# A graph-aggregation MLP layer on one core: float32 rows of h behind the gather, split on chip in batches of three chunks, the edge search and the first dense tile moved ahead of the branch

## What is computed

```
# x (3125,256) float32; 50,000 edges src -> dst, sorted by dst
h   = relu(layernorm(x))
agg = segment_sum(h[src], dst, 3125) + h
h1  = agg @ W1 + b1                       # (3125, 1024)
h1  = relu(batchnorm over the 3125 rows(h1) * gamma + beta)
out = x + relu(h1 @ W2 + b2)              # (3125, 256)
```

## Time and profile before

| | before |
|---|---|
| median of 3 runs | 427.06 us (425.68 to 458.85) |
| the profiled execution | 428.42 us, its span 426.5 us |
| mean granted TensorE clock | 0.98 |
| busy: PE, DVE, ACT, POOL | 85%, 48%, 45%, 49% of the span |
| DMA moved | 71.26 MB |

### The profile page before, as it was taken

One profiled execution on the slowest core, in us unless ns is written; L12 is line 12 of the kernel. 1 busy time (PEld: TensorE's weight loads), 2 busy tenths in 40 slices (PEclk: granted clock), 3 DMA queues, 4 the chain that ended last, 5 costly groups with the idle time before them and its releaser, 6 DMA issues.

```text
span 426.5 us, 5346 instructions
## 1 busy us (share of the span) xinstructions
PE 362.8 (85%) x1797; PEld 305.3 (72%) x1797; DVE 203.6 (48%) x513; ACT 190.1 (45%) x398; POOL 208.9 (49%) x226
## 2 busy tenths in 40 slices
PE   0103599999999999999999999945689899999995
PEld 0102488888888788888888888823468788888884
DVE  5895856546655555466555554310235521212122
ACT  1891344444444444445444443300235799991000
POOL 6580177667776767776776777774700000000000
PEclk9999999999999999999999999975999999999999
DMA  7669877767776777776676777787820003222211
GB/s 178 160 187 289 278 226 219 200 172 203 225 201 190 207 201 204 204 219 196 178 190 184 203 219 211 207 269 227 244 73 2 0 17 98 84 70 80 78 37 51
DMA packets 27054, 71.26 MB, mean 167 GB/s; under 512 B 4540, under 2 KB 11985, under 8 KB 26397
## 3 DMA queue, kind: packets, MB, share of 16 engines
q0 software_dynamic: 15504, 49.80, 40.9%
q1 hardware_dynamic: 11518, 21.06, 17.1%
HBM read 61.24 MB, written 9.60 MB: 166 GB/s over the span
## 4 chain that ended last, share of the span: by engine, by line
PE 75%; DMA 11%; POOL 5%; DVE 4%; issue 2%; ACT 2%; SPq 0%; DVEq 0%; ACTq 0%; POOLq 0%
PE ps L541 20%; PE ps L521 18%; PE ps L616 17%; PE ps L628 9%; PE ps L577 8%; DMA g_ring<-h_rows,gsrc 8%; POOL scratch L448 3%; DMA scratch<-in_src,scratch 3%; POOL g_ring L491 2%; DMA scratch<-in_x 1%; PE ps L530 1%; DVE oh L902 1%; PE ps L604 1%; ACT scratch L705 1%; DVE picks L994 0%
## 5 line engine op out<-in xcount | busy, mean ns | idle before, releaser
L491 POOL DMA_INDIRECT g_ring<-h_rows,gsrc x187 | 186.4, 997 | 90.2 <-issue 40.8
L616 PE MATMUL ps<-hp,counts 125*125 125x512 f32 x350 | 110.1, 432 | 0.0
L521 PE MATMUL ps<-hT,w 128*128 128x250 f32 (+1 forms) x416 | 98.5, 370 | 0.2
L902 DVE TENSOR_TENSOR oh<-iota,tab 128x500 bf16<-128x500 bf16 x196 | 73.4, 417 | 31.0 <-PE ps L577 30.1
L541 PE MATMUL ps<-w,h 128*125 128x256 f32 x400 | 86.7, 379 | 1.0 <-ACT h L743 1.0
L521 PEld LDWEIGHTS ps<-hT,w 128*128 128x128 f32 x416 | 76.4, 192 | 12.0 <-ACT h L678 1.1
L678 ACT ACTIVATE h<-ps,vec 128x250 f32<-128x250 f32 (+1 forms) x104 | 48.1, 463 | 81.6 <-PE ps L521 81.2
L724 ACT ACTIVATE counts<-ps 125x500 fp32r<-125x500 f32 (+1 forms) x98 | 54.7, 560 | 66.8 <-PE ps L577 65.1
L628 PE MATMUL ps<-g_ring,picks 128*125 128x512 f32 x187 | 70.2, 447 | 16.6 <-DMA g_ring<-h_rows,gsrc 14.8
L541 PEld LDWEIGHTS ps<-w,h 128*125 128x125 f32 x400 | 74.8, 188 | 12.7 <-issue 1.2
L949 DVE BATCH_NORM_STATS2 bst<-h 128x6 f32<-128x250 f32 (+1 forms) x104 | 42.5, 410 | 76.4 <-ACT h L678 75.7
(11 more groups left out here) (97 smaller groups left out, 125.3 us busy)
## 6 DMA issues: line engine op xcount, KB each, us to landing
h_rows<-hp SPq DMA_DIRECT2D x5, 1120.0 KB
x<-in_x SPq DMA_DIRECT2D x12, 250.0 KB
out<-o SPq DMA_DIRECT2D x12, 250.0 KB
g_ring<-h_rows,gsrc POOLq DMA_INDIRECT x187, 3.8
scratch<-in_x SPq DMA_DIRECT2D x5, 560.0 KB
hd<-h_rows SPq DMA_DIRECT2D x11, 224.0 KB
w<-in_L_gnn_W SPq DMA_DIRECT2D x2, 1024.0 KB, 9.0
h_rows<-hp SPq DMA_DIRECT2D x5, 130.0 KB
```

The costliest lines, as they stand in the source:

```text
L491: pool.indirect_dma_start(g_ring[:, c % GQ, :].bitcast(F32), None, h_words, bass.IndirectOffsetOnAxis(ap=gsrc[:, c:c + 1], axis=0)).then_i ...
L521: last = pe.matmul(p_hid[w % 2][:, 0:n], w1[:, f, k * P:(k + 1) * P], hT[:, buffer, f, 0:n], start=(f == 0), stop=(f == KD - 1))
L616: last = pe.matmul(p_sum[d], counts[:, d % 2, t, :], hp[:, t, :, :].rearrange("p s d -> p (s d)"), start=(t == 0), stop=(t == NT - 1))
L902: last = dve.tensor_tensor(oh[:, b % OB, v, :].rearrange("p (k g) -> p k g", g=CG), iota4[:, :, :], keys, ALU.is_equal)
```

## The change

1. `h_rows` holds one float32 row per node (1 KB instead of 2 KB). SP stores `h32`, no longer waiting for the halves. `hd`, the own rows, is float32 too and has one buffer; own rows are added by a float32 matmul after the first chunk.
2. The gather ring has 3 slots of 3 chunks (YQ, YN). A tile's 17 chunks make batches of 3, 3, 3, 3, 3, 2. ACT copies a landed batch to its rounded half (`split_hi`), DVE subtracts for the rest (`split_lo`) into `halves` (two buffers), and PE sums from there. POOL may gather batch y when batch y-3 has been split. `picks` are made per batch.
3. The search for the first edges has no gathers: all dst are loaded (125 rows of 400, and the next 100), DVE compares every 100th with the starts, PE finds the chunk and sums, DVE compares in it. The two last x loads wait no longer for it. Keys are ordered differently, so `group_keys` has four DVE operations in place of eight.
4. The order of DVE's head changes: one-hots 0 to 6 come before `gather_tables`, and the counts and dense work of slots 7 to 13 (tile 0) are run before the flag is read. POOL gathers the first 9 chunks before the flag.
5. `plan()` places splits as well as chunks. Evaluated, the new plan has 142 of 187 chunks, the same 72 units and the splits of batches 0 to 50 (of 66) in slots 0 to 104; the last chunk is in slot 124, and 90 units are placed by then. Of those 51 batches, 27 have their first chunk in the slot right after their split.

```diff
-YB = (5, 4, 4, 4)
+YB = (3, 3, 3, 3, 3, 2)
+YQ = 3
-T_ROWS, T_GATHER, T_LAND = 3500, 1250, 3700
+T_ROWS, T_GATHER, T_LAND, T_SPLIT = -6000, 1300, 3700, 2500
+EARLY = 2 * CB
...
+        while z >= EARLY and y < NG * len(YB) and len(s.splits) < 2 and (y < 2 or used.get(y - 2, z) < z):
+            free = usable[y - YQ] if y >= YQ else T_ROWS
+            landed = max(issued, free) + T_GATHER * len(chunks_of_batch(y)) + T_LAND
+            if landed > now and not idle:
                 break
...
+            usable[y] = now + T_SPLIT
...
+            if v not in usable or v in s.splits or usable[v] > now and not idle:
...
-    h_rows = nc.dram_tensor("h_rows", [N, 2 * D], F32R).ap()
+    h_rows = nc.dram_tensor("h_rows", [N, D], F32).ap()
...
+            sp.dma_start(dst_e[0:NP - 1, :], bass.AP(tensor=dst.tensor, offset=0, ap=[[EP, NP - 1], [1, EP + CE]])
+                         ).then_inc(s_dst, 16)
...
-                sp.wait_ge(s_hi, g + 1)
-                sp.wait_ge(s_lo, g + 1)
+                sp.wait_ge(s_h32, g + 1)
...
+            def gather(c):
+                y, i = batch_of_chunk(c)
+                if i == 0 and y >= YQ:
+                    pool.wait_ge(s_split, y - YQ + 1)
+                pool.indirect_dma_start(g_ring[:, y % YQ, i, :], None, h_rows, ...
...
+            for s in SLOTS[CB:EARLY]:
+                count(s.count)
+                dense(*s.dense)
...
+            def split_hi(y):
+                n = len(chunks_of_batch(y))
+                act.wait_ge(s_gath[y % YQ], landed_by(y))
+                if y >= 2:
+                    act.wait_ge(s_chunk, chunks_of_batch(y - 2)[-1] + 1)
+                act.activation(halves[:, y % 2, 0:n, 0, :], g_ring[:, y % YQ, 0:n, :], ACT.Copy).then_inc(s_ghi, 1)
...
+                    for y in s.splits:
+                        split_hi(y)
...
+            def chunks_above():
+                dve.wait_ge(s_dst, 32)
+                chain(dve.tensor_copy(nexts[:, :], ...))
+                for j in range(SB):
+                    last = dve.tensor_scalar(above[:, j, :], vrow[0:NP, :], nexts[:, j:j + 1], None, ALU.is_le)
+                dve.tensor_tensor(steps[:, :, :]..., dst_e[:, 0:EP], dst_e[:, CE:EP + CE], ALU.subtract)
+            def smaller():
+                dve.scalar_tensor_tensor(less[:, :], p_rows, PAD_DST, vrow[0:CE, :], ALU.add, ALU.is_lt)
...
+                def split_lo(y):
+                    dve.wait_ge(s_ghi, y + 1)
+                    dve.tensor_tensor(halves[:, y % 2, 0:n, 1, :], g_ring[:, y % YQ, 0:n, :],
+                                      halves[:, y % 2, 0:n, 0, :].bitcast(F32), ALU.subtract).then_inc(s_split, 1)
```

More of the change, by code:

```diff
@@ L94, in chunks_of_batch, with landed_by @@
     return range(a, a + YB[v])
+def landed_by(y):
+    return 16 * sum(len(chunks_of_batch(v)) for v in range(y % YQ, y + 1, YQ))
 def plan():
@@ L112, in plan @@
     tiles, blocks, ready, todo, placed = [], [], {}, [], 0
-    used = []
-    z, now, c, gate, landed = CB, 0, 0, 0, T_ROWS + T_LAND
+    z, now, c, gate = CB, 0, 0, EARLY
+    y, issued, used, usable = 0, T_ROWS, {}, {}
     while placed < UNITS:
@@ L117, in plan @@
         finished = []
-        while c < NC and z >= gate and len(s.chunks) < 4:
-            if z < end and landed > now:
+        idle = z >= end and not todo
+        while z >= EARLY and y < NG * len(YB) and len(s.splits) < 2 and (y < 2 or used.get(y - 2, z) < z):
+            free = usable[y - YQ] if y >= YQ else T_ROWS
+            landed = max(issued, free) + T_GATHER * len(chunks_of_batch(y)) + T_LAND
+            if landed > now and not idle:
                 break
             now = max(now, landed)
+            issued = landed - T_LAND
+            s.splits.append(y)
+            usable[y] = now + T_SPLIT
+            y += 1
+        while c < NC and z >= gate and len(s.chunks) < 4:
+            v = batch_of_chunk(c)[0]
+            if v not in usable or v in s.splits or usable[v] > now and not idle:
+                break
+            now = max(now, usable[v]) + T_CHUNK
             s.chunks.append(c)
-            used.append(now)
+            used[v] = z
             c += 1
@@ L157, in plan @@
         z += 1
+        if z == EARLY:
+            now = 0
     assert blocks[-3:] == list(range(NBLK - 3, NBLK)), blocks
-    for y in range(NG * len(YB)):
-        z = CB if y < 2 else next(i for i, s in enumerate(slots) if chunks_of_batch(y - 1)[0] in s.chunks)
-        at(z).picks.append(y)
+    for v in range(NG * len(YB)):
+        z = EARLY if v < 2 else next(i for i, s in enumerate(slots) if chunks_of_batch(v - 1)[0] in s.chunks)
+        at(z).picks.append(v)
     return slots, tiles, blocks
+FIRST_C = chunks_of_batch(YQ)[0]
 SLOTS, TILES, BLOCKS = plan()
@@ L235, in build @@
         vrow = cut(LANES)
[L236 to L247, removed]
+        vrow_r = cut(GROUPS)
+        dst_e = cut(EP + CE, NP).bitcast(I32)
+        nexts = cut(SB, NP)
         win_i = cut(WB).bitcast(I32)
@@ L666, in _ @@
                     for s in range(n):
[L667 removed]
+                        last = pe.matmul(ps[0:NP, s, 0:D], zeros, g_any[:, 4 + s, :], start=False, stop=True)
                     last.then_inc(s_gclose, 1)
@@ L781, in _ @@
                     for s in range(n):
-                        copy_low(act, tiles + s, ps[0:NP, s, :])
+                        act.activation(low[:, :], ps[0:NP, s, 0:D], ACT.Copy).then_inc(s_low, 1)
                         if m:
@@ L1006, in _ @@
                         onehots(s.count + OB)
+                    for y in s.splits:
+                        split_lo(y)
                     for y in s.picks:
```

350 lines of the change are left out of this document (174 added, 176 removed).

## The result

The changed kernel takes **441.92 us** (median of 4, 440.42 to 443.99) against 427.0 of the kernel before on the same chip: ratio **1.0376** [1.0343, 1.0409], slower. Ratios here compare fast executions alone (of the four of before, the one of 458.85 us was in the chip's slower state), so they aren't exactly the quotient of the medians. The profiled execution took 440.42 us with a span of 438.6, 12.1 more than before. The forecast of 433 had the sign and missed 9 us of the size: 441.92 lies inside the stated 422 to 446, but above the 427 to 439 of the forecast itself.

A forecast was written before the change was run, and what follows sets the result against it. PE was taken as the bound from 50.04 to 279.6 us, then gathers. Dense end 279.6 - 6.6 + 1.5 - 5.0 + 4 = 273.5, plus 55.5 and 13.0 to 342.0, plus 90.9: span 432.9, time 433 us, range 422 to 446.

The forecast's parts named there:

- the forecast itself: The case in which the forecast's own steps hold: 427 to 439 us, chance 0.48.
- The head: Before dense work: without search gathers and with half the store, dense work starts at 43.4 us, 6.6 earlier.
- The bubble: Slots 7 to 13 and slot 14: cover sum, the flag's matmul and the branch add 1.5 us (0 to 3).
- The middle: Slots 0 to 104: 20 fewer chunks give -5.0 us, waits for the new splits +4 (0 to 13).
- one own-rows matmul fewer, 0.4: Slots 0 to 104: a saving of 0.4 us on PE, counted within the -5.0 for fewer chunks.
- DVE and ACT become the clock of the middle: Rival, chance 0.17: split chain too long in 27 tight batches; PE waits 13 to 20 us, not 4: 443 to 449.
- Behind slot 104: After the last dense matmul: 36 gathers at POOL's 1.25 us each make the stretch 55.5 us (50 to 62).
- The end: Last gather to last chunk summed: landing 2.6, hi and lo of two chunks 1.5, two matmuls 0.5 us.
- the change delivers its gain: Rival, chance 0.17: head 10 earlier, no bubble or split waits, 50 us behind slot 104: 418.5; half of each, 423.
- The port rule "in full": Rival, chance 0.10: behind slot 104 splits and picks hold gathers throughout, 18 us instead of 4: 447; with half, 440.
- The early search: Rival, chance 0.08: the early search doesn't move the dense start, which comes only 2 us earlier: 437.5.
- a smaller row buys "nothing": Gathers behind slot 104: POOL's pace stays 0.95 + 0.30 us each, so halving the row gains nothing.

The follow-up runs named there:

- r5: The kernel before with only the new edge search, head order and tile 0 before the flag; old 2 KB rows and ring, no splits: 424.91 us, ratio 0.9974.
- r1: The kernel before with one planner constant changed (T_GATHER 1250 to 1500), so 135 chunks instead of 162 in slots 0 to 104: 445.85 us, ratio 1.0439.
- r9: The changed kernel with T_LAND 2700 and T_SPLIT 3500: still 142 early chunks, but 5 tight batches instead of 27: 436.02 us, ratio 1.0244.
- r4: The changed kernel without DVE's subtraction for the low half (left zero); POOL and PE wait for ACT's copy instead: 430.4 us, ratio 1.0099.
- r8: r3 with picks made by one DVE operation with one SBUF tensor input per chunk, instead of one two-input operation per batch: 428.7 us, ratio 1.0067.
- r7: The kernel before, each gather fetching only the rounded halves (1 KB a row), low halves zero; order, ring, store and head unchanged: 423.61 us, ratio 0.9932.
- r3: The changed kernel with T_ROWS -11000, T_LAND 2200, T_SPLIT 3500: 151 early chunks instead of 142, 2 tight batches instead of 27: 428.54 us, ratio 1.0055.

## Why the prediction missed its size

**The head held.** Dense work starts at 43.13 for a forecast of 43.4. Two terms erred against each other: the load of all dst landed at 7.54, not 5.0, and DVE's chain with its waits took 35.6 us instead of 37.8 plus the count. The bubble of +1.5 put into slots 7 to 13 and the branch didn't come (9.91 us, before 9.83). r5 shows what the head is worth alone: 4.8 us of start, 3.5 of span, and by the median 1.6 us, which its interval doesn't tell from none.

**The middle is the step that failed**: "New are per batch ... I take 0.15 each: +4 (0 to 13)", against -5.0 for the 20 chunks. The single operations were priced within 0.05 us, and DVE is at 72% (159.77 of 223.26) for a forecast of 77. What was wrong is the sum. The chunks were worth more than taken, 0.33 each by r1, so -6.6; from slot 14 on the stretch grew by 3.4 instead of shrinking, so what the change adds there is 10.0 us, not 4. Only 5.0 of them are waits that the view shows (6.8 less 1.8). The other five lie inside what the rows count as busy, where ends are modelled: PE's busy time is 216.44 for 20 chunks fewer, 217.66 before. Some 1.1 of them are a term that the forecast had with the wrong sign, "one own-rows matmul fewer, 0.4": in float32 the own rows of nine tiles are 18 matmuls and 5.4 us busy (L607), where those of ten were 10 matmuls and 4.7 us (L604).

r9 and r4 say where more of the ten comes from: room between split and chunk takes 4.3 us off, leaving out `split_lo` takes 4.2 off, and both end at 219.0. By r1's price 142 chunks without splits would be at 213.3; 5.7 are left in each. PE's waits there are 4.6 us in r9 (3.9 for picks) and 4.5 in r4 (3.5 for picks), 2.8 and 2.7 more than before; the own rows are 1.1; the last 1.8 or so have no experiment of their own, and stay open.

The rival "DVE and ACT become the clock of the middle" described this mechanism, in tight batches. It set 13 to 20 us for it and came too high, as the forecast came too low; the time stands between them. The sign that the forecast named for it, PE waiting over 8 us for splits, didn't show: by the view it waits 6.8, and the rest of the cost isn't seen as waits.

**Behind slot 104** the decisive step held: 57.6 us for 55.5, gathers at POOL's pace. Of its terms: 37 gathers started there, not 36; their stretch over 0.947 us is 2.8 us, not 4; to the end of the last gather it is 50.5 us, where 36 at 1.25 with the stretch, the start and the stretched landing made 51.0. The 6.69 us landing came as expected and cost POOL 1.3 beyond its 0.30. The end was too short: "landing 2.6, hi and lo 1.5, two matmuls 0.5", 4.6 us, against 7.07, since the last splits stood behind units, in part at half clock. After the last chunk 13.7 us for 13.0, the rest 91.0 for 90.9.

**The sum.** Against 433.4: head -0.3, slots 7 to 13 -1.5, middle +4.6, tail +2.1, units +0.7, rest and outside the span about 0; that is, to 0.1, the 440.4 of the profiled execution less 434.8. That the profiled execution stands only 5.6 us off is in part luck: head and bubble erred by 1.8 the other way. The last 2.9 us are the step from it to the median: this profiled execution was the fastest of the four (440.42, median 441.92), where the forecast carried over the ratio of before and took 1.4 off.

**The other rivals.** That the change delivers its gain fell with the tail, as r1 makes plain (its 418.5 was a span; with the forecast's own steps to a time it is 419). The port rule "in full" isn't there in size: gathers under `split_lo` are held for nearly the rest of it, but behind slot 104 all stretch together is 2.8 us for a price of 18, since only 9 of the 37 gathers start under one. r8 shows besides that freeing one operation gives nothing when gathers then meet the next. The early search, with the rest of the new head, did move the dense start. That a smaller row buys "nothing" was a little off: the pace is unchanged, but POOL waits less for the ring (in the tail never over 0.30 us at a time; before, 3.8 us in all beyond the 0.30), and r7 gained 0.7%.

**No version beats the kernel before clearly.** The new head on the old rows (r5, 424.91) is within what can be told; r7 is 0.7% faster but leaves the low halves of the gathered rows out. In the changed scheme the best was r3, 428.54. A deeper ring for the batches, which might let POOL run ahead of the splits, wasn't tried.

## What to carry to other kernels

Where a serial engine with a fixed cost per instruction (here 1.25 us a gather on POOL) feeds a stage, count what a new order or a smaller ring leaves behind the last work that can hide it, and price each piece by what isn't hidden: here 0.7 us a chunk. That count gives the size of the loss, but add up the other stages too: here a gain at the head and a cost of the splits hid each other. Halving bytes brings next to nothing for such a cost (0.7% in r7), and a step put between transfer and use costs its latency wherever the consumer is due in the next slot, though every engine has spare time by its busy share. When a planner with constants places the work, a change of the kernel and a change of the plan arrive together; retune the constants on both sides before the change itself is judged (13.4 of 14.9 us here).

## What the runs showed of the hardware

- A gather is held by a two-input float32 DVE operation under which it starts for all but about 0.13 us of what is left of it (0.62 for 0.75, 0.18 for 0.31), by bfloat16 one-hots in part only (4.0 us of 9.7), and not by a one-input comparison (0.03 us over 32 gathers). The order in which they start decides, and removing one such operation moved the gathers under another.
- A gather of 128 rows takes POOL 0.95 + 0.30 us for 1 KB rows as for 2 KB rows; only the median landing falls, from 3.8 to 2.8 us (r7).
- In r3 the granted clock of the middle was 0.98, where it is 1.00 in the changed kernel. Two slices of 15 us hold it, in which PE was busy 13.2 and 13.3 us. It is worth some 3 us of full clock (twice 0.11 of 15), so r3's stages aren't quite those of an even clock. Stretches of r3:

```profile
52.00:67.00 15.00, 13.23 (x67) 10.87 (x66) 9.76 (x22) 6.77 (x13) 7.41 (x9) 0.89 0.25 75
...
82.00:97.00 15.00, 13.26 (x62) 10.96 (x61) 8.62 (x21) 7.42 (x15) 8.19 (x10) 0.89 0.30 88
```
